# First attention of an eight-layer sandwich: all queries projected and rotated in a stage of their own, over 16 pairs of heads, kept in DRAM as float32 and loaded head by head

## The reference

```python
q = _rmsnorm(hidden_states @ Wq_a, q_a_ln_w) @ Wq_b          # rank 192, then 32 heads x (128 + 64)
q_nope, q_pe = (q[..., :NOPE], q[..., NOPE:])
ckv = hidden_states @ Wkv_a
compressed, k_pe = (ckv[..., :KV_RANK], ckv[..., KV_RANK:])  # 64 and 64, k_pe the same for all heads
kv = _rmsnorm(compressed, kv_a_ln_w) @ Wkv_b
k_nope, v = (kv[..., :NOPE], kv[..., NOPE:])
q_pe = _apply_rope(q_pe, cos, sin)
k_pe = _apply_rope(k_pe, cos, sin)
scores = jnp.einsum('bhqd,bhkd->bhqk', qf, kf) * scale       # qf = [q_nope, q_pe], kf = [k_nope, k_pe]
scores = jnp.where(causal, scores, jnp.finfo(scores.dtype).min)
probs = jax.nn.softmax(scores, axis=-1)
o = jnp.einsum('bhqk,bhkd->bhqd', probs, v)
return o.transpose(0, 2, 1, 3).reshape(b, s, H * VD) @ Wo
```

## Time and profile before

| | |
|---|---|
| median of 3 runs | 2994.73 us (2982.85 to 3002.94) |
| the profiled execution | 2989.91 us, its span 2987.7 us |
| busy: PE, PEld, DVE, ACT, POOL | 2557.8 (86%), 1325.8 (44%), 1596.8 (53%), 1257.1 (42%), 633.4 (21%) us |
| DMA | 99.79 MB, mean 33 GB/s |

### The profile page before, as it was taken

The page is one execution under the profiler, slowest core; times in us unless marked ns, Lnnn a source line. Parts: engine busy times, 40 slices in busy tenths (PEclk is TensorE's granted clock), DMA queues, the critical chain, the costliest instruction groups (busy, mean ns, idle before and its releaser), DMA issues. The chain is left out here.

```text
span 2987.7 us, 37616 instructions
## 1 busy us (share of the span) xinstructions
PE 2557.8 (86%) x12992; PEld 1325.8 (44%) x12992; DVE 1596.8 (53%) x2703; ACT 1257.1 (42%) x1756; POOL 633.4 (21%) x506
## 2 busy tenths in 40 slices
PE   4999999999999797739999995759999996999757
PEld 3566666666666573313332322323333323444434
DVE  3555555555556335457777746337787753011253
ACT  3444545444555422214565672214655663010331
POOL 1345444444545302310000002110000001001021
PEclk8899998989999998869999997879999998999778
DMA  2011111111011120120100000340111101100001
GB/s 63 17 34 34 38 37 27 37 34 37 27 43 31 66 72 21 61 69 1 28 14 15 14 1 15 91 99 1 38 28 23 22 1 57 71 0 0 16 0 53
DMA packets 72090, 99.79 MB, mean 33 GB/s; under 512 B 34392, under 2 KB 42840, under 8 KB 69680
## 3 DMA queue, kind: packets, MB, share of 16 engines
q1 hardware_dynamic: 71984, 98.27, 11.4%
HBM read 77.14 MB, written 20.84 MB: 33 GB/s over the span
## 5 line engine op out<-in xcount | busy, mean ns | idle before, releaser
L1937 POOL TENSOR_TENSOR l0a_p_low<-yT,l0a_p_high 128x1024 fp32r<-128x1024 f32 (+7 forms) x256 | 379.9, 1489 | 478.4 <-ACT l0a_p_high L1999 478.4
L1431 DVE TENSOR_REDUCE l2a_mx<-ps 128x1 f32<-128x512 f32 x512 | 338.1, 689 | 126.5 <-PE ps L1272 124.8
L1431 DVE TENSOR_REDUCE l1a_mx<-ps 128x1 f32<-128x512 f32 x512 | 337.0, 688 | 112.7 <-PE ps L1272 110.6
L1398 ACT ACTIVATE l2a_prob<-ps 128x1024 f32<-128x1024 f32 x256 | 250.7, 1019 | 131.7 <-PE ps L1311 93.8
L1398 ACT ACTIVATE l1a_prob<-ps 128x1024 f32<-128x1024 f32 x256 | 250.7, 1019 | 130.3 <-PE ps L1311 93.7
L1986 ACT ACTIVATE yT<-ps 128x1024 f32<-128x1024 f32 (+7 forms) x256 | 166.0, 648 | 276.2 <-PE ps L1869 174.8
L2052 DVE TENSOR_REDUCE l0a_mx<-ps 128x1 f32<-128x512 f32 (+3 forms) x384 | 203.9, 552 | 125.6 <-PE ps L1849 122.1
L1272 PE MATMUL ps<-l1a_k,l1a_q 96*128 96x512 bf16 x512 | 199.6, 399 | 65.0 <-DMA l1a_k<-l1a_k_parts 47.8
L173 POOL TENSOR_TENSOR applied<-prepared,neghalf 128x2 f32<-128x2 f32 x64 | 58.3, 911 | 900.3 <-DVE prepared L154 900.3
L1272 PE MATMUL ps<-l2a_k,l2a_q 96*128 96x512 bf16 x512 | 193.3, 391 | 46.4 <-DMA l2a_k<-l2a_k_parts 34.1
L1999 ACT CAST l0a_p_high<-yT 128x1024 fp32r<-128x1024 f32 (+7 forms) x256 | 172.0, 672 | 7.1
(11 more groups left out here) (291 smaller groups left out, 4570.0 us busy)
## 6 DMA issues: line engine op xcount, KB each, us to landing
l0a_woh<-in_l0a_wo SPq DMA_DIRECT2D x32, 256.0 KB, 2.6
l0a_cos_recip<-l0a_recip_row SPq DMA_DIRECT2D x32, 256.0 KB, 3.7
l0a_o<-l0a_o_pair SPq DMA_DIRECT2D x16, 512.0 KB, 2.7
yT<-l0a_o SPq DMA_DIRECT2D x16, 512.0 KB, 3.2
...
```

The source lines that it names most:

```text
L1398: nc.scalar.activation(prob[:, s % (2 * GROUP), :], ST[s % 2].rearrange("p b n -> p (b n)"), ACT.Exp, scale=SCALE).then_inc(s_exp, 1)
L1431: nc.vector.tensor_reduce(mx[:, m // NT, m % NT, c:c + 1], MB[c], AX.X, ALU.max).then_inc((s_red0, s_red1)[c], 1)
L1937: nc.gpsimd.tensor_tensor(p_low[:, j % 4, P * j:T], prob[:, j % 4, P * j:T], p_high[:, j % 4, P * j:T], ALU.subtract).then_inc(s_pl, 1)
```

## The change

`mla_heads` loses jobs 0 to 3 and all that belonged to them. They move into a new Block, `mla_queries`, ahead of it, which walks over 16 pairs of heads. Per pair it projects the rotary rows of both heads as one 128-row tile and the latent rows as another. The three high/low products of each contraction part become five of 128 contraction rows (the 64 rows left over from 192 are stacked, high above low, in `pe_rest` and `ab_rest`). ScalarE and VectorE bring the rotary rows out of PSUM, GpSimd multiplies and adds, and two DMAs store the pair as float32 into `q_dram` (32 heads x 128 rows x 1024). `latents` also loads all rotary weights and splits them. In the head loop a query is one DMA of 512 KB per head; ScalarE casts it at the end of the head two before, and VectorE instead of GpSimd makes its low part (`rest`). `PLAN` places only the twelve maximum products; the turn stands in step 4. Elsewhere in `split_qk` a few semaphores are only made where they are used.

The diff, cut to its core:

```diff
--- before.py
+++ after.py
...
         o_dram = nc.dram_tensor("l0a_o", (PAIRS, P, T), F32).ap()
-        with ExitStack() as temp:
-            latents(chip, temp, add_f, a, qT0, qT1, kT, k_high, k_low, cext)
         s_in = [chip.sem(f"l0a_o_loaded{i}") for i in range(3)]
         s_stored = chip.sem("l0a_o_stored")
-        with ExitStack() as temp:
-            mla_heads(chip, temp, a, qT0, qT1, k_high, k_low, cext, o_dram, wo, s_in, s_stored)
+        q_dram = nc.dram_tensor("l0a_q", (MLA_HEADS, P, T), F32).ap()
+        with ExitStack() as both:
+            q32 = both.enter_context(nc.sbuf_tensor("l0a_q32", [P, 2, T], F32))
+            s_q = [chip.sem(f"l0a_q_loaded{i}") for i in range(2)]
+            with ExitStack() as parts:
+                pe_high, pe_low, pe_rest = (
+                    parts.enter_context(nc.sbuf_tensor("l0a_" + n, [P, MLA_HEADS * ROPE], F32R))
+                    for n in ("pe_high", "pe_low", "pe_rest"))
+                with ExitStack() as temp:
+                    latents(chip, temp, add_f, a, qT0, qT1, kT, k_high, k_low, cext, pe_high, pe_low, pe_rest)
+                with ExitStack() as temp:
+                    mla_queries(chip, temp, a, qT0, qT1, pe_high, pe_low, pe_rest, q_dram, wo, q32, s_q)
+            with ExitStack() as temp:
+                mla_heads(chip, temp, a, k_high, k_low, cext, q_dram, q32, s_q, o_dram, s_in, s_stored)
...
+        for dst, rows in ((pe0, slice(0, P)), (pe1, slice(P, Q_RANK))):
+            sp.dma_start(dst[:].rearrange("r (h c) -> r h c", h=MLA_HEADS),
+                         a["l0a_wqpe"][:, rows].rearrange("h r c -> r h c")).then_inc(s_pe_in, 16)
...
+            nc.scalar.copy(pe_high[:], pe0[:]).then_inc(s_pe_high, 1)
+            nc.scalar.copy(pe_rest[0:64, :], pe1[:]).then_inc(s_pe_high, 1)
             for t in range(NT):
...
+            dve.wait_ge(s_pe_high, 1)
+            nc.vector.tensor_tensor(pe_low[:], pe0[:], pe_high[:], ALU.subtract)
+            dve.wait_ge(s_pe_high, 2)
+            nc.vector.tensor_tensor(pe_rest[64:128, :], pe1[:], pe_rest[0:64, :], ALU.subtract)
...
+def mla_queries(chip, mem, a, qT0, qT1, pe_high, pe_low, pe_rest, q_dram, wo, q32, s_q):
...
+    wv, woh = sb("wvT", [P, SLOTS, 2, KV_RANK]), sb("woh", [P, SLOTS, 2, D])
+    ab_high, ab_low, ab_rest = sb("ab_high", [P, P], F32R), sb("ab_low", [P, P], F32R), sb("ab_rest", [P, P], F32R)
+    q_lat, q_pe = sb("q_lat", [P, 2, T]), sb("q_pe", [P, 2, T])
+    straight, turned = sb("straight", [P, 2, T]), sb("turned", [P, 2, T])
+    s_ld = [chip.sem(f"l0q_weights{i}") for i in range(SLOTS)]
+    s_st = [chip.sem(f"l0q_stored{i}") for i in range(2)]
+    s_c = chip.sem("l0q_tables")
+    s_pe, s_act, s_dve, s_pool = (chip.sem("l0q_" + n) for n in ("products", "act_done", "dve_done", "rotated"))
+    LAT, AB, VO = ps[:, 0:2, :], ps[:, 6, :], ps[:, 7, :]
+    def pe_banks(p):
+        return ps[:, 2 + 2 * (p % 2):4 + 2 * (p % 2), :]
+    def wide(banks):
+        return banks.rearrange("p b n -> p (b n)")
+    def absorbed_at(p):
+        return 4 * p if p else 1
+    def vo_at(p):
+        return 4 * p + (5 if p + 1 < PAIRS else 4)
+    def high_at(p):
+        return 6 * p + 4 if p else 5
...
+    with nc.Block() as block:
+        @block.sync
+        def _(sp):
+            def load(p):
+                def ld(dst, src):
+                    sp.dma_start(dst, src).then_inc(s_ld[p % SLOTS], 16)
+                two = slice(2 * p, 2 * p + 2)
+                ld(wqn[:, p % SLOTS], a["l0a_wqnT"][two].rearrange("h p r -> p h r"))
+                ld(wk[:, p % SLOTS], a["l0a_wkT"][two].rearrange("h p r -> p h r"))
+                ld(wv[:, p % SLOTS], a["l0a_wvT"][two].rearrange("h p r -> p h r"))
+                ld(woh[:, p % SLOTS], a["l0a_wo"][two].rearrange("h p r -> p h r"))
+            def store(p):
+                two = q_dram[2 * p:2 * p + 2]
+                sp.wait_ge(s_act, 6 * p + 8)
+                sp.dma_start(two[:, 0:KV_RANK, :], q_lat[:, p % 2, :]).then_inc(s_st[p % 2], 16)
+                sp.wait_ge(s_pool, 2 * p + 2)
+                sp.dma_start(two[:, KV_RANK:P, :], q_pe[:, p % 2, :]).then_inc(s_st[p % 2], 16)
+            load(0)
+            for i in range(2):
+                sp.dma_start(cos[64 * i:64 * i + 64, :], a["l0a_cosT"]).then_inc(s_c, 16)
+                sp.dma_start(sin[64 * i:64 * i + 64, :], a["l0a_sinT"]).then_inc(s_c, 16)
+            load(1)
+            load(2)
+            for p in range(PAIRS):
+                store(p)
+                if p + SLOTS < PAIRS:
+                    sp.wait_ge(s_pe, vo_at(p))
+                    load(p + SLOTS)
+            sp.wait_ge(s_st[0], 32 * (PAIRS // 2))
+            sp.wait_ge(s_st[1], 32 * (PAIRS // 2))
+            for i in range(2):
+                sp.dma_start(q32[:, i, :], q_dram[i]).then_inc(s_q[i], 16)
+        @block.tensor
+        def _(pe):
+            def absorb(p):
+                s = p % SLOTS
+                pe.wait_ge(s_ld[s], 64 * (p // SLOTS + 1))
+                for i in range(2):
+                    nc.tensor.matmul(AB[:, 64 * i:64 * i + 64], wqn[:, s, i, 0:P], wk[:, s, i, :], start=True, stop=True)
+                    mm = nc.tensor.matmul(AB[0:64, P + 64 * i:P + 64 * i + 64], wqn[:, s, i, P:Q_RANK], wk[:, s, i, :],
+                                          start=True, stop=True)
+                mm.then_inc(s_pe, 1)
+            def project(banks, high, low, rest):
+                for c in range(2):
+                    cut = slice(512 * c, 512 * c + 512)
+                    nc.tensor.matmul(banks[:, c, :], high, n_high[:, 0, cut], start=True, stop=False)
+                    nc.tensor.matmul(banks[:, c, :], high, n_low[:, 0, cut], start=False, stop=False)
+                    nc.tensor.matmul(banks[:, c, :], low, n_high[:, 0, cut], start=False, stop=False)
+                    nc.tensor.matmul(banks[:, c, :], rest, n_high[:, 1, cut], start=False, stop=False)
+                    mm = nc.tensor.matmul(banks[:, c, :], rest, n_low[:, 1, cut], start=False, stop=True)
+                return mm
+            absorb(0)
+            pe.wait_ge(s_act, 3)
+            pe.wait_ge(s_dve, 3)
+            for p in range(PAIRS):
+                s = p % SLOTS
+                pair = slice(P * p, P * p + P)
+                if p >= 2:
+                    pe.wait_ge(s_act, 6 * p - 5)
+                    pe.wait_ge(s_dve, 5 * p - 2)
+                project(pe_banks(p), pe_high[:, pair], pe_low[:, pair], pe_rest[:, pair]).then_inc(s_pe, 1)
+                pe.wait_ge(s_act, high_at(p))
+                pe.wait_ge(s_dve, 5 * p + 5)
+                project(LAT, ab_high[:], ab_low[:], ab_rest[:]).then_inc(s_pe, 1)
+                if p + 1 < PAIRS:
+                    absorb(p + 1)
+                if p:
+                    pe.wait_ge(s_act, 6 * p + 5)
+                for i in range(2):
+                    mm = nc.tensor.matmul(VO[64 * i:64 * i + 64, :], wv[:, s, i, :], woh[:, s, i, :],
+                                          start=True, stop=True)
+                mm.then_inc(s_pe, 1)
+        @block.scalar
+        def _(act):
+            def absorbed(p):
+                act.wait_ge(s_pe, absorbed_at(p))
+                nc.scalar.copy(ab_high[:], AB[:, 0:P]).then_inc(s_act, 1)
+                nc.scalar.copy(ab_rest[0:64, :], AB[0:64, P:2 * P]).then_inc(s_act, 1)
+            nc.scalar.copy(n_high[:, 0, :], qT0).then_inc(s_act, 1)
+            for i in range(2):
+                nc.scalar.copy(n_high[64 * i:64 * i + 64, 1, :], qT1[0:64, :]).then_inc(s_act, 1)
+            absorbed(0)
+            for p in range(PAIRS):
+                act.wait_ge(s_pe, 4 * p + 2)
+                if p >= 2:
+                    act.wait_ge(s_pool, 2 * p - 2)
+                raw = wide(pe_banks(p))
+                for i in range(2):
+                    nc.scalar.copy(turned[32 * i:32 * i + 32, p % 2, :], raw[32 - 32 * i:64 - 32 * i, :]).then_inc(s_act, 1)
+                act.wait_ge(s_pe, 4 * p + 3)
+                if p >= 2:
+                    act.wait_ge(s_st[p % 2], 32 * (p // 2))
+                nc.scalar.copy(q_lat[:, p % 2, :], wide(LAT)).then_inc(s_act, 1)
+                if p + 1 < PAIRS:
+                    absorbed(p + 1)
+                act.wait_ge(s_pe, vo_at(p))
+                nc.scalar.copy(wo[:, p, :], VO).then_inc(s_act, 1)
+        @block.gpsimd
+        def _(pool):
+            pool.wait_ge(s_c, 64)
+            for p in range(PAIRS):
+                b = p % 2
+                pool.wait_ge(s_act, 6 * p + 7)
+                nc.gpsimd.tensor_tensor(turned[0:64, b, :], turned[0:64, b, :], sin[0:64, :], ALU.mult).then_inc(s_pool, 1)
+                pool.wait_ge(s_pool, 2 * p + 1)
+                pool.wait_ge(s_dve, 5 * p + 8)
+                if p >= 2:
+                    pool.wait_ge(s_st[b], 32 * (p // 2))
+                nc.gpsimd.tensor_tensor(q_pe[:, b, :], straight[:, b, :], turned[:, b, :], ALU.add).then_inc(s_pool, 1)
```

(131 more changed lines are left out.)

222 lines of the change are left out of this document (67 added, 155 removed).

## The result

The changed kernel takes 3076.36 us (median of 4 runs, 3074.61 to 3080.98) against 2998.84 (4 runs, 2982.85 to 3014.05): 1.0262 times the time before, 95% interval 1.0205 to 1.0318. It is slower, by 78 us; forecast were 3091 us. The profiled execution took 3080.98 us, 91 more than the profiled one of before.

A forecast was written before the change was run, and what follows sets the result against it. TensorE's own work was taken to bound the head loop. Profiled 2989.9 us + 367 (new stage, bound by stores on two DMA engines) - 271 (shorter loop) = 3086, or 3091 for the median; range 3030 to 3170.

The forecast's parts named there:

- What bounds the loop: Head loop before: TensorE's own work bounds it, 28.76 us a head, slowed by mixed 64-row and 128-row products and half clock.
- The loop after: Head loop without the projection: 20.3 us a head at full clock, 655 us in all, 271 us less.
- The split of the stalls: TensorE's waits per head in the changed loop: 0.6 us for ScalarE's exponential, 0.4 us for VectorE's maxima.
- The stores: New stage: two heads outermost put each store on two of 16 DMA engines, 20.5 us a pair, 16 pairs.
- The loads: New stage: weight loads also pass the stores' two DMA engines, 3.0 us a pair for 13 pairs.
- The start: `latents`: its additional casts and 1.5 MB load lie under TensorE's products, price 0; without that cover 4 to 10 us.
- TensorE in the stage: New stage: TensorE's products take 7.6 us a pair, 122 us for 16 pairs, hidden under the stores.
- rival A: New stage: stores use all 16 DMA engines, so TensorE's 7.6 us a pair bounds it; kernel 2840 us, chance 0.09.
- The weight loads' row groups: TensorE: rejected the rule that a weight load overlaps a running product only if their row groups differ.
- B: Head loop gains less, from a falling clock or adding stalls: 23.6 us a head, kernel 3193 us, chance 0.06.
- C: New stage: each pair's stores wait for earlier ones to land, 2 us more a pair; 3123 us, within the forecast's 0.85.

The follow-up runs named there:

- experiment 4: The kernel before, with the projection's 64-row products filled up to 128 rows by rows of zeros: 2925.16 us, 0.9767 times before.
- experiment 1: The changed kernel with each two-head store of the new stage cut into two DMAs of one head (64 rows outermost): 2834.3 us, 0.946 times before.
- experiment 5: The changed kernel with `q_dram` turned so each store, as many as before, has 128 rows outermost; a head loaded by two DMAs: 2830.3 us, 0.9455 times before.
- experiment 7: The changed kernel with each pair's stores four outermost (32 rows each, places in DRAM 33 rows apart): 2918.35 us, 0.9767 times before.
- experiment 3: The changed kernel without the weight loads of pairs 3 to 15, which use the first three pairs' weights: 3044.16 us, one run.
- experiment 2: The changed kernel with only `q_lat`'s stores cut by head, the rotary rows keeping the two-head store: 2936.46 us, one run.

## Why the prediction was right

Forecast 3091, measured 3076; against the profiled execution 3086 and 3081. The mechanism was as forecast, but that the profiled execution is hit within 5 us is in part luck: the first scores came 16 us earlier than forecast (445.4 for 462), the loop was right, and the rest of the kernel, at which nothing was forecast, took 11 us more. Step by step:

- **What bounds the loop.** Right, and tested by experiment 4 apart from the change: clock and spacing of the projection's products were as read.
- **The loop after.** 20.3 us a head forecast, 20.29 measured, 655 us in all forecast and 655.4 measured, clock 1.00. The sum was not closed: 19.1 + 0.6 + 0.4 is 20.1, and nothing is given for the other 0.2. The split of the stalls was off as well: the trace shows 0.3 us a head for ScalarE's exponential (forecast 0.6), and for VectorE's maxima 32.0 us of waiting weight loads, or 1.2 a head in 27 heads, beside 20.9 of waiting products, 0.8, which may be the same time (forecast 0.4). Taken together TensorE was idle for 28 of the 655 us, 0.9 a head against 1.0 allowed, so the misses about cancel.

```profile
PEld ps L2014 <- DVE l0a_mx L2167: 32.0, 54, 0.8
PE ps L2014 <- DVE l0a_mx L2167: 20.9, 54, 0.6
PEld ps L2034 <- ACT yT L2120: 9.1, 27, 0.4
```

- **The stores.** Two of 16 engines: right (experiments 1, 5 and 7). 20.5 us a pair forecast, 19.88 measured (experiment 3), the lower of the two rates I had; 16 x 0.6 = 10 us too much. The rule cited from the Trainium skill (DMA: Bandwidth & Descriptors) gave the same numbers of engines, and the trace agrees for 2 (53 GB/s, share 0.13) and 4 (105 GB/s, share 0.26).
- **The loads.** 3.0 us a pair forecast, 2.3 measured: 13 x 0.7 = 9 us too much. The two together are the stage's surplus, less some 3 us at its ends: I had the last store end at 442, it ended by 426.66; from there to the first scores 20 us were forecast and 18.8 measured. In the steady pairs of experiments 2 and 7 the same 2.3 us turn up.
- **The start.** `latents` with its additional casts and loads cost nothing, as forecast: the first load of the new Block is issued at 57.6 us, like that of the head loop's Block before.
- **TensorE in the stage.** 7.6 us forecast for a pair, 6.8 measured where it bounds (experiment 1). I took 1.90 us for `wv` times `wo` of one head from a row at half clock and counted half of it for each head; experiment 4 has the 1.04 us of one head at full clock. But two heads write two column halves of the same bank, and their products overlap: all four pieces together run in about 1.1 us.

```profile
122.56 0.64 PE L1829 MATMUL ps<-l0q_woh,l0q_wvT 128*64 128x512 f32 x1
...
122.71 1.02 PE L1829 MATMUL ps<-l0q_woh,l0q_wvT 128*64 128x512 f32 x3
...
123.67 0.50 PE L1801 MATMUL ps<-l0q_n_high,l0a_pe_high 128*128 128x512 f32 x1
```

(from experiment 1). Under the stores this cost nothing; without them it is 16 x 0.8 = 13 us, which accounts for rival A's price, 2840, being 6 to 10 us too high: with 16 engines the kernel takes 2830 to 2834.
- **The weight loads' row groups.** I had rejected the Trainium skill's rule (TensorE: Matmul & The Clock Gate, Part 3) on the spacing of equal products. Experiment 4 bears this out: products on the same 128 rows stand 0.23 us apart, and making all alike halved the projection. What the mixed ones wait for is not shown by any run.
- **Rivals.** B is refuted by 20.29 us and the clock; C by the 19.88 us of experiment 3, at 52.8 GB/s the rate of stores that follow each other without a gap; A described what the change becomes once the stores are laid out otherwise.
- **Not forecast at all:** that SyncE's issues would take up to 9.8 us, and that TensorE would wait for weights. Both lay under the stores.
